# Turning the int8 levels of each tile by a transposing DMA instead of TensorE, with six of eight samples rounded on ScalarE

## What is computed

```
conv = conv1d(x, weight, kernel 9, padding 4, 4 groups)        # x: 64 x 64 x 1024
c    = conv + (cond @ c_weight.T)[:, :, None] + bias[None, :, None]
aq   = fake_quant(c, 8 bits, per row of 1024)                  # absmax / 127, round, times scale
kq   = fake_quant(kernel, 8 bits, per output column)           # 1024 x 1024
y    = aq @ kq + fake_quant(bias2, 16 bits)
out  = x + fake_quant(y, 8 bits, per row)
```

## Time and profile before

| | |
|---|---|
| Time, median of 3 runs | 280.97 us (279.25 to 282.17) |
| Profiled execution: its own time | 278.56 us |
| Profiled execution: span | 276.7 us |
| Mean granted TensorE clock | 0.986 of full |
| Busy: TensorE, VectorE, ScalarE, GpSimd | 251.1, 238.8, 185.2, 153.8 us |
| Mean DMA traffic | 203 GB/s |

### The profile page before, as it was taken

The page is one execution under the profiler, slowest core; times in us unless marked ns, Lnnn a source line. Parts: engine busy times, 40 slices in busy tenths (PEclk is TensorE's granted clock), DMA queues, the critical chain, the costliest instruction groups (busy, mean ns, idle before and its releaser), DMA issues.

```text
span 276.7 us, 4240 instructions
## 1 busy us (share of the span) xinstructions
PE 251.1 (91%) x1372; PEld 163.5 (59%) x1372; DVE 238.8 (86%) x509; ACT 185.2 (67%) x278; POOL 153.8 (56%) x71
## 2 busy tenths in 40 slices
PE   7866769999999999999999999999999999997540
PEld 3555557666666666666666666666666666663210
DVE  1799964799999999999999999999999989999984
ACT  6257586477777777777777777777777767564762
POOL 2533333356666666666666666666666666533453
PEclk9979999999999999999999999999999999999996
DMA  6997322406666565566666766666666663333355
GB/s 253 416 408 301 123 84 103 153 0 227 223 203 212 211 202 212 203 217 217 209 204 210 230 228 228 228 227 226 219 203 197 218 218 117 144 142 139 107 220 219
DMA packets 15799, 56.04 MB, mean 203 GB/s; under 512 B 1954, under 2 KB 1954, under 8 KB 15778
## 3 DMA queue, kind: packets, MB, share of 16 engines
q1 hardware_dynamic: 15488, 55.71, 56.8%
q10 hardware_dynamic: 290, 0.07, 0.1%
HBM read 38.99 MB, written 16.78 MB: 202 GB/s over the span
## 4 chain that ended last, share of the span: by engine, by line
PE 81%; DVE 8%; ACT 4%; DMA 3%; issue 2%; SPq 0%; DVEq 0%
PE dense_ps L427 36%; PE conv_ps L396 31%; PE turn_ps L416 5%; PE conv_ps L386 5%; DMA k_raw<-ffn_kernel 3%; DVE dense_ps L550 2%; DVE y L559 2%; DVE y_max L604 2%; ACT kq L279 2%; PE small_ps L407 2%; PE dense_ps L449 1%; DVE k_max L523 1%; ACT a_int L304 1%; PE dense_ps L440 1%; ACT x_hi L265 1%
## 5 line engine op out<-in xcount | busy, mean ns | idle before, releaser
L427 PE MATMUL dense_ps<-kq,a_t 128*128 128x512 bf16 x512 | 120.6, 379 | 6.1 <-DVE y L559 5.0
L218 POOL TENSOR_TENSOR x_lo<-xwin,x_hi 128x1032 fp32r<-128x1032 f32 x32 | 76.6, 2393 | 80.8 <-ACT x_hi L265 80.8
L227 POOL TENSOR_TENSOR o_sb<-y,o_sb 128x1024 f32<-128x1024 f32 x31 | 73.9, 2384 | 32.8 <-ACT y L315 32.7
L427 PEld LDWEIGHTS dense_ps<-kq,a_t 128*128 128x128 bf16 x512 | 48.9, 101 | 53.7 <-issue 6.7
L295 ACT CAST a_t<-turn_ps 128x1024 bf16<-128x1024 int16 x32 | 32.4, 1012 | 48.5 <-PE turn_ps L416 48.5
L564 DVE TENSOR_REDUCE small_ps<-conv_ps 128x8 f32<-128x1024 f32 x32 | 39.4, 1232 | 13.8 <-PE conv_ps L396 13.5
L550 DVE SCALAR_TENSOR_TENSOR dense_ps<-dense_ps,row_scale,k_scale_b 128x512 f32<-128x512 f32 x64 | 47.7, 745 | 3.6 <-PE dense_ps L427 3.6
L312 ACT ACTIVATE y_int<-y,y_inv 128x1024 int16<-128x1024 f32 x31 | 35.6, 1148 | 22.3 <-DVE y_inv L611 22.1
L559 DVE TENSOR_TENSOR y<-dense_ps,bq 128x512 f32<-128x512 f32 x64 | 43.9, 685 | 2.8 <-ACT bq L288 1.6
L604 DVE TENSOR_REDUCE y_max<-y 128x1 f32<-128x1024 f32 x32 | 38.7, 1210 | 0.7 <-issue 0.2
L304 ACT ACTIVATE a_int<-conv_ps,inv 128x128 int16<-128x128 f32 x128 | 36.0, 363 | 1.1 <-DVE inv L590 1.1
(11 more groups left out here) (55 smaller groups left out, 160.2 us busy)
## 6 DMA issues: line engine op xcount, KB each, us to landing
xwin<-x_windows SPq DMA_DIRECT2D x32, 516.0 KB, 4.8
o_sb<-x_rows SPq DMA_DIRECT2D x32, 512.0 KB, 5.3
out<-o_sb SPq DMA_DIRECT2D x31, 512.0 KB, 2.9
k_raw<-ffn_kernel SPq DMA_DIRECT2D x4, 1024.0 KB, 10.5
w_raw<-taps SPq DMA_DIRECT2D x2, 256.0 KB, 3.2
b_row<-ffn_bias SPq DMA_DIRECT2D x1, 512.0 KB, 15.9
out<-o_sb SPq DMA_DIRECT2D x2, 256.0 KB, 2.7
condt<-cond_t ACTq DMA_DIRECT2D x1, 32.0 KB
```

What stands on the lines that cost most here:

```text
L218: pool.tensor_tensor(x_lo[:, at].rearrange("p n b -> p (n b)"), xwin[:, t % XWIN, :], x_hi[:, at].bitcast(F32).rearrange("p n b -> p (n b) ...
L227: pool.tensor_tensor(o_sb[:, at, :], y[:, t % YRING, :], o_sb[:, at, :], ALU.add).then_inc(s["o_made"], 1)
L427: mm = pe.matmul(dense_ps[:, h, :], a_t[:, t % LEVELS, q].rearrange("b j o -> b (j o)"), kq[:, q, half(h)], start=(q == 0), stop=(q == Q - 1))
```

## The change

The levels are no longer turned by TensorE. SP issues one transposing DMA for each tile (`turn_levels` on SP), which reads `a_int` in SBUF and writes `a_turn`, a new int16 buffer of two tiles in SBUF. `take_levels` on ScalarE waits for that DMA and casts from `a_turn`. `turn_ps` and TensorE's eight transposes of each tile go. VectorE rounds two samples instead of four, and ScalarE six instead of four (its samples 2 and 3 come last, behind a wait for VectorE's share). TensorE's order is the same in all iterations now.

```diff
+DVE_N = 2
+        a_turn = sb("a_turn", [P, 2, NS, P], I16)
-        turn_ps = ps("turn_ps", [P, NS, P], I16)
...
+            def turn_levels(t):
+                at = t % 2
+                sp.wait_ge(s["a_rounded_dve"], t + 1)
+                sp.wait_ge(s["a_rounded"], t + 1)
+                wait(sp, "a_made", t - 1)
+                sp.dma_start_transpose(out=a_turn[:, at], in_=a_int[:, at, :]
+                                       ).then_inc(turned[at], 16)
...
                 if there(k - TAIL + 2):
                     load_x(k - TAIL + 2)
+                if there(k - 1):
+                    turn_levels(k - 1)
                 if 0 <= k - TAIL - 1 < LAST:
                     store(k - TAIL - 1)
...
             def take_levels(t):
-                wait(act, "a_turned", t + 1)
+                act.wait_ge(turned[t % 2], nth(t, 2))
...
                 act.copy(a_t[:, t % LEVELS].rearrange("b q j o -> b j q o"),
-                         turn_ps[:].rearrange("b j (q o) -> b j q o", q=Q)
+                         a_turn[:, t % 2].rearrange("b j (q o) -> b j q o", q=Q)
...
             def round_levels(t):
                 at = t % 2
                 wait(act, "inv_made", t + 1)
-                wait(act, "a_turned", t - 1)
-                for n in range(NS // 2, NS):
+                if t > 1:
+                    act.wait_ge(turned[at], nth(t - 2, 2))
+                for n in (*range(NS // 2, NS), *range(DVE_N, NS // 2)):
+                    if n == DVE_N:
+                        wait(act, "a_rounded_dve", t + 1)
...
-            def turn_levels(t):
-                wait(pe, "a_rounded_dve", t + 1)
-                wait(pe, "a_rounded", t + 1)
-                wait(pe, "a_made", t)
-                for j in range(NS):
-                    mm = pe.transpose(turn_ps[:, j, :].bitcast(BF16),
-                                      a_int[:, t % 2, j * BLOCKS:(j + 1) * BLOCKS].bitcast(BF16),
-                                      ident_b[:])
-                mm.then_inc(s["a_turned"], 1)
...
-                wait(dve, "a_turned", t - 1)
-                half_n = NS // 2
+                if t > 1:
+                    dve.wait_ge(turned[at], nth(t - 2, 2))
+                half_n = DVE_N
```

More of the change, by code:

```diff
@@ L112, in build @@
             "hi_made", "lo_made", "conv_made", "col_max_made", "col_max_masked",
-            "max_spread", "row_max_made", "scale_made", "picked_made", "inv_made", "a_rounded", "a_rounded_dve", "a_turned",
+            "max_spread", "row_max_made", "scale_made", "picked_made", "inv_made", "a_rounded", "a_rounded_dve",
             "a_made", "dense_made0", "dense_made1", "scaled0", "scaled1", "biased0", "biased1",
@@ L118, in build @@
         k_in = [sem(f"k_in{i}") for i in range(KB // 2)]
+        turned = [sem(f"turned{i}") for i in range(2)]
         x_in = [sem(f"x_in{i}") for i in range(ORING)]
@@ L473, in _ @@
                     k_turns(7, 8)
-                if k in (2, 3, TILES):
+                if there(k - LAG[0]):
                     dense(k - LAG[0], 0)
[L476 to L483, removed]
-                    spread_max(k)
[L485 to L494, removed]
+                if k == 2:
+                    k_turns(5, 6)
+                if there(k):
+                    spread_max(k)
+                if there(k - LAG[1]):
+                    dense(k - LAG[1], 1)
         @block.vector
@@ L591, in levels @@
                 wait(dve, "inv_made", t + 1)
-                wait(dve, "a_turned", t - 1)
-                half_n = NS // 2
-                dve.tensor_tensor(a_int[:, at, 0:HALF].rearrange("p (n b) -> p n b", b=BLOCKS),
+                if t > 1:
+                    dve.wait_ge(turned[at], nth(t - 2, 2))
+                half_n = DVE_N
+                dve.tensor_tensor(a_int[:, at, 0:half_n * BLOCKS].rearrange("p (n b) -> p n b", b=BLOCKS),
                                   conv_cols(at)[:, 0:half_n, :],
```

## The result

| | before | after |
|---|---|---|
| Time, median | 281.29 us (279.25 to 282.17, 4 runs) | 332.71 us (329.19 to 333.08, 4 runs) |
| Profiled execution: its own time, span | 278.56, 276.7 us | 332.97, 331.1 us |
| Mean granted TensorE clock | 0.986 | 0.953 |

The ratio is 1.183, 95% interval 1.174 to 1.192: slower, inside the stated range, and 18 us under the likeliest value of 351.

The account below looks back on a forecast made before the run. TensorE bounds the kernel before at 7.33 us a tile; afterwards ScalarE's loop would, at 5.80 + T. The sum 227 + 31 T with T = 4.0 gave 351 us, range 311 to 460.

Parts of the forecast that it names:

- The mechanism: ScalarE's in-order loop: the cast waits for the transposing DMA with nothing ahead to hide it; a tile takes 5.80 + T.
- ScalarE's work: ScalarE, start of cast to end of last rounding: 5.80 us a tile, with six roundings at 1.65.
- T: End of the last rounding to landing of the transposing DMA: 2.5 + 1.0 + 0.5 = 4.0 us, bounds 2.7 and 10.5.
- 227 + 31 T: Whole kernel: the forecast time in us as a function of the DMA wait, each microsecond of it costing 31 us.
- case A: Transposing DMA: the forecast itself, T from 3.2 to 5.0, 326 to 382 us, likeliest 351; chance 0.45.
- B: Transposing DMA as cheap as a plain one: T 2.5 to 3.2, 305 to 326 us; chance 0.18.
- The share of the moved roundings: ScalarE: the two roundings taken over from VectorE cost 32 x 0.52 = 17 us of the forecast time.
- What hides T: ScalarE's order: nothing found to hide T; TensorE has slack, the dense product being due a tile later.
- SP's queue: Transposing DMA behind two loads and ahead of the store on SP: costed at nothing, up to 2.4 us if tiles were shorter.
- case E: TensorE's clock: 2.4 GHz expected throughout; otherwise 105 us more, about 456; chance counted within the slow-DMA rival's 0.30.

Follow-up runs that it names:

- the plain copy: The kernel after, with an ordinary 256 KB DMA from SBUF to SBUF in place of the transposing one, the turning left out: 306.1 us.
- doubled: The kernel after, with each transposing DMA issued twice, the first copy to a spare buffer nobody reads: 376.42 us.
- run 1: The kernel after, with ScalarE's cast of the turned levels moved behind the split and the output rounding: 275.7 us, ratio 0.980 to before.
- run 2: The kernel after, with the roundings put back to four samples on VectorE and four on ScalarE: 317.65 us.
- run 9: Late-cast kernel, cast moved behind the roundings: 291.4 us; also TensorE's small product later: 290.62; instead the dense product's first half a tile later: 275.58.

## Why the prediction was right

**The mechanism** held. The time of a tile is ScalarE's work and T, and by the roundings the sum can be checked: forecast 5.80 + T, measured 5.77 + 3.13; with four samples 5.26 + 3.13; with the plain copy 5.77 + 2.41; doubled 5.77 + 4.52. Hiding T (run 1) is the counter-proof. 3.34 us, the mean of the 32 waits, in 227 + 31 T gives 330.5, and the profiled execution took 333.

**The term that was mis-sized** is T: 4.0 forecast, 3.13 in an undisturbed tile. I had 2.5 us fixed, 1.0 of moving and 0.5 for a longer issue. Fixed are 1.1 + 0.7 = 1.8; the plain copy inside SBUF (2.3 with its 0.65) has 1.65 left, about as much. I had read the 2.5 from stores to HBM. The moving takes 1.25. The issue does hold SP for 1.23 us, but the data start 1.1 us after its beginning as with a plain copy, so it costs T nothing. The typical T falls a little below the bounds of case A and into B; with the long tiles the mean wait is in A. By the typical T alone the sum is 227 + 31 x 3.13 = 324 us. What lifts the time to 333, into the bounds of A, is mostly the late landings, on which the prediction says nothing; that much of the agreement is luck, though 324 lies in the stated range too.

**ScalarE's work**: cast 1.04 for the 1.05 expected, six roundings 1.64 for 1.65. The share of the moved roundings was put at 17 us, run 2 measured 15.

**What hides T:** I found nothing in the order as it stood, and the 107 us of waits confirm it. That TensorE has slack for a cast that is late was said too loosely; run 9 showed half a microsecond with the late cast, and in the kernel after TensorE itself waited for the casts 24 times, 30.1 us in all.

**SP's queue** cost nothing in an undisturbed tile: the wait of 3.13 is the landing of 3.05 and the signals. Once, at 152.52 us, the issue itself came 0.5 us late.

**The clock** (case E) fell in some stretches, which I hadn't expected. The first of them in the loop lies behind a late DMA, in whose shadow TensorE waited 2.48 us for the cast:

```profile
91.86 3.39 PE L432 MATMUL dense_ps<-kq,a_t 128*128 128x512 bf16 x8 [2.48 <-ACT a_t L307]
...
89.00:92.00 3.00, 0.53 (x3) 0.13 (x2) 2.55 (x3) 1.24 (x2) 0.00 (x0) 0.92 1.01 326
92.00:94.00 2.00, 2.00 (x6) 0.64 (x5) 0.35 (x3) 1.97 (x3) 1.17 (x1) 0.50 0.39 160
95.00:98.00 3.00, 3.00 (x17) 1.97 (x16) 2.65 (x9) 1.53 (x6) 2.56 (x2) 1.00 0.07 14
```

TensorE was busy in 0.53 of 3 us, and in the next 2 us, though busy all the time, it was granted 0.50, the level of 1.2 GHz; from 95 us on it had 1.00, 2.4 GHz. The half of the dense product in this stretch took 3.39 us, where it takes 1.90 at the full clock. The next cast of ScalarE, at 100.31, came 9.55 us after the one before, all of it beyond 8.90 in its own DMA wait (3.79 for 3.13): TensorE's lost time fell into its slack.

## What to carry to other kernels

Before work is moved to a queue or an engine with latency, look at what stands behind the instruction that waits for it: here 0.46 us of a bound engine was saved and 3.1 us put into the in-order loop of another, which then ruled. The same DMA gains 2% when two other steps of the waiting engine stand between its issue and its use, and loses 18% when none does; put its use neither before it lands nor later than the next engine needs the result. And a share of work moved to the less busy engine costs in full once that engine's own loop is the bound.

## What was not expected of the hardware

**The issue of a transposing DMA hardly depends on its size.** 1.19 us on SP's queue for 128 KB and 1.23 for 256 KB, the two sizes run, against 0.47 for a plain copy inside SBUF and, in the kernel before, 0.34 for a store.

**A packet of instructions and a late landing come together.** 8 of the 32 casts of the kernel after waited 3.7 to 5.0 us. The traffic from 226 us on, where a transpose was issued at 225.22 and landed 4.5 us later, and the traffic from 86.5 us on, where one was issued at 85.86 and landed 4.9 us later:

```profile
GB/s 0 0 0 236 211 213 205 178 102 18 0 0 0 0 2 8 8 10 8 10 10 188 287 287 476 328 492 524 524 328 295 426 524 66 393 66 264 397 462 297
...
q8 instruction: 1, 0.02, 1.8%
...
GB/s 0 0 0 0 84 213 225 215 205 217 217 195 195 193 527 451 135 600 295 328 393 492 492 98 360 165 264 330 231 330 363 297 396 264 429 396 329 230 296 328
...
q8 instruction: 1, 0.02, 1.2%
```

In the first, the traffic stops after some 0.8 us for 1.4 us but for about 10 GB/s; then transpose and store go on. One packet of the instruction queue q8, 0.02 MB, begins near 226.4, and its 1.8% of 16 engines' 5 us are 1.4 us of one engine. In the second the packet begins near 88.7, when the transpose has all but moved: the traffic behind it goes on, and the landing is late all the same. Of the eight late casts six have such a packet in the flight of their DMA, near 88, 125, 189, 226, 263 and 300 us, and landings of 4.0 to 4.9 us; the traffic stops for a microsecond or more in the four between 125 and 263. The seventh has a packet of 0.01 MB from queue q14, near 98 us, and a landing of 3.7. The eighth is the one whose issue was 0.5 us late, with packets of q14 near 151 to 153 us. The q8 packet near 159 us lies between two flights, and no cast waited longer for it.

With the plain copy one of the seven q8 packets from 60 us on fell in while the data of a copy moved: that copy landed after 4.3 us, but the traffic behind it went on at 260 to 480 GB/s before it paused for 0.7 us. A stop in the middle of the transfer is thus seen only with the transposing DMA. That the instruction packet is the cause is inferred from the coincidence; no run removed it. The waits beyond 3.13 us of the eight casts add up to about 10 us of the 51.
